# Down products of a feed-forward in seven half-width products instead of eight full-width tiles, in the last two of four sweeps

## The chip, the cores and the metric

The kernel runs on one core of a Trainium2 chip. The metric is the device time of one execution in microseconds; the median of several runs is compared. A profiled execution is one of its own, with its own time.

## The reference

For 8 x 512 tokens of 512 channels, in f32: attention with 16 heads of 32 channels (causal, softmax), added to its input and normalised over the channels; then a gated feed-forward, again added and normalised:

```python
gate = xt @ Wg.T ; up = xt @ Wu.T          # 4096 hidden values, weights unpacked from 4-bit codes and scales
gelu = tanh(0.7978845608 * (gate + 0.044715 * gate**3)) * gate * 0.5 + gate * 0.5
out = (gelu * up) @ Wd.T                   # back to 512 channels
```

## The kernel before

**Work and tiles.** An attention phase runs first, batch by batch, and the feed-forward phase overlaps its tail. The feed-forward is `feed_forward_phase`, and the change lies in it alone. It goes over the 4096 tokens in 4 sweeps (`NS`) of 1024 tokens (two tiles t of 512), and in each sweep over the 4096 hidden values in 16 groups (`NG`) of 256 (two halves m of 128). One group in one sweep is a quad, numbered j = 0 to 63; sweeps 3 and 4 are j = 32 to 47 and 48 to 63. In sweep 1 the weights of each group are unpacked, split in a high and a low float32r part and written to `w_scratch`; in the later sweeps they are read back from there.

**Precision.** Every product of f32 matrices is three matmuls in float32r (`three`, lines 1036 to 1040): high by high, high by low, low by high. A matmul has its own weight load.

**Gate and up** are made by a seven-product scheme for 2 x 2 blocks: 7 products per matrix and quad (`p1` to `p7`), each over two halves of the 256 + 256 input channels, so six matmuls of 512 columns, 84 for both matrices. Sums of input blocks (`sum_x`, `x_next`) and of weights (`sum_w`) are made beforehand; ACT copies banks between products (`seed`, `take_u2`, `take_u3`) and DVE adds them (`make_c22`, `seed_e`). ACT then does the gelu into `hid` (four blocks of 128 x 512, index 2m + t), DVE multiplies by up in place (`times_up`, hid_done), ACT copies the product to its float32r high part (`split_high`, inter_high) and POOL subtracts it to get the low part (`split_low`, inter_split).

**Down.** The down product of quad j - 1 is made during quad j (`down`, lines 1087 to 1107): for each of 8 subtiles of 128 tokens, six matmuls of 512 columns (two halves m, three passes), stationary `inter`, moving `wd`, into one of two banks `d_bank[n % 2]`. It waits for the low parts of its tokens, for the weights, and for DVE to have added the tile two before into the accumulator `acc` (`add_down`, lines 1421 to 1429, d_added).

**Order.** Each engine's order is written out by hand in its `rest()`, one pass of the loop for each quad; engines meet only at semaphores. PE's pass is:

```python
p1(j, "g"), p1(j, "u"), down(j - 1, 0), p6(j, "g"), p2(j, "g"), p6(j, "u"), p2(j, "u"), down 1, down 2,
p7, p5 "g", down 3, p7, p5 "u", down 4, p4 "g", p4 "u", down 5, p3 "g", p3 "u", down 6, down 7
```

(lines 1139 to 1161). SP issues all transfers (`rest`, lines 992 to 1031): in pass j, once all products of quad j - 1 are done, `wg` and `wu` of quad j + 1, and once the down product of quad j - 2 is done, `wd` of quad j + 1 (1 MB). At the first two quads of a sweep DVE takes the statistics of the finished tokens (`statistics`, `refine`), POOL normalises them to `out_stage`, and SP stores them and loads the residual of the next tokens to `acc`. At the last quad of a sweep (j % 16 == 15) DVE, ACT and POOL make the next sweep's inputs (`sum_x`, `x_part`, `x_low`).

## Time and profile before

| | us |
|---|---|
| median of 3 runs (lowest, highest) | 2690.54 (2690.24, 2692.3) |
| the profiled execution | 2689.03 |
| its span, first to last instruction | 2687.2 |
| PE busy (share of the span) | 2629.9 (98%) |
| DVE busy | 1555.0 (58%) |
| ACT busy | 1103.5 (41%) |
| POOL busy | 825.7 (31%) |
| mean granted clock of PE, share of full | 0.993 |

Busy time is a sum over an engine's instructions, over all stages. Matmuls are pipelined: one of 512 columns is shown with 0.39 us while the next starts sooner, so the interval between starts is the measure of the pace. PEld is the weight load, which runs beside matmuls.

### The profile page before, as it was taken

What the parts mean: (1) busy time and instruction counts of PE and PEld (TensorE: products, weight loads), DVE (VectorE), ACT (ScalarE), POOL (GpSimd) and SP (SyncE); (2) the same over time, 40 slices, a digit from 0 to 9 for tenths busy, and PEclk for the clock granted to TensorE, in tenths of its full rate; (3) what the DMA queues carried; (4) which work ended last, traced back from release to release, by engine and by line L of the source; (5) the groups of instructions that cost most, each with busy time, mean ns of one, the idle gap of its engine ahead of it and who ended that gap; (6) DMA issues with size and microseconds to landing.
All of it is one profiled execution on the core that took longest, in us unless ns stands there. A gap on an engine that the chain in (4) does not pass through costs nothing.

```text
span 2687.2 us, 37714 instructions
## 1 busy us (share of the span) xinstructions
PE 2629.9 (98%) x13314; PEld 2148.2 (80%) x13314; DVE 1555.0 (58%) x3224; ACT 1103.5 (41%) x2518; POOL 825.7 (31%) x992
## 2 busy tenths in 40 slices
PE   7999999999789999999999999999999999999998
PEld 6777887778468888888888888888888888888886
DVE  5777777777789888876333333633333363333334
ACT  4666666666644444443222222322222232222221
POOL 2444444443634443434111111321111132111112
PEclk9999999999899999999999999999999999999999
DMA  9666876768365655565444333554344345433441
GB/s 251 188 178 178 215 212 174 190 187 233 105 250 216 225 208 204 205 262 232 163 180 189 156 141 145 210 201 172 143 182 169 141 160 229 167 141 141 182 171 48
DMA packets 143085, 493.52 MB, mean 184 GB/s; under 512 B 11568, under 2 KB 48560, under 8 KB 118320
## 3 DMA queue, kind: packets, MB, share of 16 engines
q1 hardware_dynamic: 142896, 491.11, 53.2%
q8 instruction: 106, 1.74, 0.3%
q14 instruction: 83, 0.68, 0.1%
HBM read 356.84 MB, written 134.22 MB: 183 GB/s over the span
## 4 chain that ended last, share of the span: by engine, by line
PE 71%; DVE 1%; DMA 1%; issue 1%; ACT 0%; POOL 0%; SPq 0%; POOLq 0%; DVEq 0%; ACTq 0%
PE bank L1038 23%; PE bank L1039 23%; PE bank L1040 23%; PE bank L452 0%; DMA scale<-down_scales 0%; DMA x1T_scratch<-x_late 0%; DVE bstats L1486 0%; PE bank L438 0%; DVE acc L1429 0%; ACT probs L562 0%; PE bank L462 0%; PE bank L419 0%; ACT bx_h L1169 0%; DVE bits L1389 0%; DVE y L708 0%
## 5 line engine op out<-in xcount | busy, mean ns | idle before, releaser
L1648 POOL TENSOR_TENSOR inter_l<-hid,inter_h 128x512 fp32r<-128x512 f32 x256 | 338.0, 1321 | 1361.5 <-ACT inter_h L1169 1361.5
L1429 DVE TENSOR_TENSOR acc<-acc,bank 128x512 f32<-128x512 f32 x512 | 350.0, 685 | 331.8 <-PE bank L1040 322.8
L1038 PE MATMUL bank<-wd,inter_h 128*128 128x512 f32 x1024 | 399.7, 390 | 6.2 <-DVE acc L1429 5.2
L1039 PE MATMUL bank<-wd,inter_h 128*128 128x512 f32 x1024 | 398.9, 390 | 0.0
L1040 PE MATMUL bank<-wd,inter_l 128*128 128x512 f32 x1024 | 398.9, 390 | 0.0
L743 POOL TENSOR_SCALAR probs<-probs,row_inv 128x128 f32<-128x128 f32 (+3 forms) x512 | 264.4, 538 | 363.1 <-DVE row_inv L664 363.1
L1448 DVE TENSOR_TENSOR hid<-hid,bank 128x512 f32<-128x512 f32 x192 | 131.8, 687 | 397.1 <-PE bank L1040 395.4
L1038 PE MATMUL bank<-bx_h,wg 128*128 128x512 f32 x896 | 349.4, 390 | 0.9 <-ACT u_g L1169 0.9
L1039 PE MATMUL bank<-bx_l,wg 128*128 128x512 f32 x896 | 349.1, 390 | 0.0
L1040 PE MATMUL bank<-bx_h,wg 128*128 128x512 f32 x896 | 349.1, 390 | 0.0
L1038 PE MATMUL bank<-bx_h,wu 128*128 128x512 f32 x896 | 348.7, 389 | 0.0
L1040 PE MATMUL bank<-bx_h,wu 128*128 128x512 f32 x896 | 348.6, 389 | 0.0
L1039 PE MATMUL bank<-bx_l,wu 128*128 128x512 f32 x896 | 348.5, 389 | 0.0
L562 ACT ACTIVATE probs<-probs,neg_max 128x128 f32<-128x128 f32 (+3 forms) x512 | 281.7, 556 | 0.0
L675 DVE CUSTOM_DVE_ANT_0 probs<-bank,mask 128x128 f32<-128x128 f32 (+3 forms) x512 | 243.9, 481 | 26.2 <-PE bank L430 21.6
L1169 ACT ACTIVATE inter_h<-hid 128x512 fp32r<-128x512 f32 x256 | 160.6, 628 | 220.1 <-PE bank L1040 119.9
L438 PE MATMUL bank<-ident,probs 128*128 128x128 f32 x1280 | 228.3, 278 | 13.9 <-POOL probs L743 6.2
L1038 PEld LDWEIGHTS bank<-wd,inter_h 128*128 128x128 f32 x1024 | 192.5, 188 | 48.7 <-issue 5.3
L1237 ACT ACTIVATE hid<-bank 128x512 f32<-128x512 f32 x192 | 114.7, 597 | 269.7 <-PE bank L1040 197.3
L1040 PEld LDWEIGHTS bank<-wd,inter_l 128*128 128x128 f32 x1024 | 192.5, 188 | 40.1
L1039 PEld LDWEIGHTS bank<-wd,inter_h 128*128 128x128 f32 x1024 | 192.5, 188 | 39.6
L430 PE MATMUL bank<-k_st,q_st 128*128 128x256 f32 (+2 forms) x512 | 209.8, 410 | 12.4 <-DVE neg_max L675 7.0
(139 smaller groups left out, 4357.9 us busy)
## 6 DMA issues: line engine op xcount, KB each, us to landing
wg<-w_scratch SPq DMA_DIRECT2D x48, 1792.0 KB, 9.0
wu<-w_scratch SPq DMA_DIRECT2D x48, 1792.0 KB, 12.9
wd<-w_scratch SPq DMA_DIRECT2D x48, 1024.0 KB, 4.9
q_st<-qk_scratch SPq DMA_DIRECT2D x128, 256.0 KB, 5.0
k_st<-qk_scratch SPq DMA_DIRECT2D x128, 256.0 KB, 6.9
w_scratch<-wg SPq DMA_DIRECT2D x16, 1792.0 KB, 8.2
w_scratch<-wu SPq DMA_DIRECT2D x16, 1792.0 KB, 10.0
qk_scratch<-q_stage SPq DMA_DIRECT2D x32, 512.0 KB, 3.6
```

The lines of the kernel that those rows point to most:

```text
L430: pe.matmul(s_bank[k % 2][:, 0:n], q_st[:, st, g, k * P:(k + 1) * P], k_st[:, st, g, 0:n], start=True, stop=True).then_inc(s_done, 1)
L438: last = pe.transpose(t_bank[k % 2][:, (i - k) * P:(i - k + 1) * P], probs[:, h % 4, PCOL[i] + k * P:PCOL[i] + (k + 1) * P], ident[:])
L562: act.activation(p, p, ACT.Exp, bias=neg_max[:, h % 4, k:k + 1], scale=-1.0, accum_out=row_sum[:, h % 4, k:k + 1]).then_inc(exp_done, 1)
L675: dve.tensor_tensor_reduce(probs[:, s % 4, PCOL[k]:PCOL[k] + n], s_bank[k % 2][:, 0:n], mask[:, SEQ - n:SEQ], -SCALE, 3.0e38, ALU.add, ALU ...
L743: pool.tensor_scalar(p, p, row_inv[:, h % 4, k:k + 1], 1.0, ALU.mult, ALU.mult).then_inc(norm_done, 1)
L1038: pe.matmul(out, a(0), b(0), start=start, stop=False, skip_group_check=True)
L1039: pe.matmul(out, a(0), b(1), start=False, stop=False, skip_group_check=True)
L1040: return pe.matmul(out, a(1), b(0), start=False, stop=stop, skip_group_check=True)
L1169: return act.activation(out, in_, ACT.Copy)
L1429: dve.tensor_tensor(a, a, d_bank[n % 2][:, :], ALU.add).then_inc(d_added, 1)
L1448: dve.tensor_tensor(h, h, u_of(m, t), ALU.mult).then_inc(hid_done, 1)
L1648: pool.tensor_tensor(inter[1][:, m, t, :], hid[:, 2 * m + t, :], f32(inter[0][:, m, t, :]), ALU.subtract).then_inc(inter_split, 1)
```

## The change

In 28 quads, those with `seven(j)` (j = 33 to 46 and 49 to 62), the down product is made by the seven-product scheme too. Its 2 x 2 blocks are: tokens t by hidden halves m on one side, hidden halves m by halves of the 512 output channels on the other. Each product i has one hidden operand (128 x 512 tokens) and one weight operand (128 x 256). A step is one product for 256 tokens: two token tiles, each with three matmuls of 256 columns, into the two halves of one bank. Steps 0 to 6 are products 0 to 6 for the first 256 tokens of each tile, steps 7 to 13 for the second. A bank accumulates over steps where `FRESH` doesn't start it anew: products share partial sums in PSUM, and each step's bank is added to the accumulator's half rows that `ADD_TO` names.

- PE does the steps in pairs between pairs of products (`with_steps`).
- DVE makes four sums of hidden blocks (`hidden_sums`, around the adds of steps 12 and 13) and adds 14 steps; ACT and POOL split seven operands in high and low parts (`operand_high`, `operand_low`) where four were split.
- The four sums of down weights are made once, in sweep 2 (14 quads, `summed(j)`): POOL adds the two parts and makes the sums (`sums_of_down`), ACT and POOL split them, SP stores 1 MB for each to a new scratch `t_scratch` (`store_t`).
- In sweeps 3 and 4 SP loads seven weight operands of 256 KB for each such quad into `b_slot` (over `wd`), each when its slot is free (`load_operands`), in place of 1 MB of `wd`. `wd` of other quads is loaded one pass later than before (`load_down`).
- `sum_x` is cut in four calls, which DVE places between adds in quad 47. Other tiles lie over buffers that are idle then.

The core of the diff (the semaphores, the waits of `gelu`, and the rest of the orders, which follow the same pattern, are left out):

```diff
+HALF = HID // 2
+ADD_TO = ((0, 0), (0, 0), (0, 1), (1, 1), (1, 1), (0, 1), (1, 0))
+FRESH = (0, 1, 3)
+WEIGHT_OF = {0: (0, 0), 1: (1, 0), 5: (1, 1)}
+SUM_OF = {2: 0, 3: 1, 4: 2, 6: 3}
+PLACE_OF = {(0, 0): 0, (1, 0): 1, (0, 1): 4, (1, 1): 6}
...
+    spare = [plan(f"spare{n}", [P, TILE], F32R) for n in range(3)]
+    d_whole = plan("d_whole", [P, 2, HID], F32, over="w32_d")
+    t_sum = plan("t_sum", [P, 4, HALF], F32, over="spare0")
+    t_parts = plan("t_parts", [P, 4, 2, HALF], F32R, over="out_stage")
...
+    s1_parts = [plan(f"s1_{n}", [P, TILE], F32R, over="w32_d", skip=4 * TILE * i) for i, n in enumerate("hl")]
+    s4_low = plan("s4_l", [P, TILE], F32R, over="wd_0", skip=3 * 8 * HALF)
+    hid_sum = plan("hid_sum", [P, 2, TILE], F32, over="w_sum_g")
+    b_slot = [plan(f"b_slot{i}", [P, 2, HALF], F32R, over="wd_1" if i < 4 else "wd_0", skip=i % 4 * 8 * HALF)
+              for i in range(7)]
...
+    def seven(j):
+        return j >= 2 * NG and 0 < j % NG < NG - 1
+    def summed(j):
+        return j - NG if NG < j < 2 * NG - 1 else 0
+    def whole_loads(j):
+        return (j - NG) // 2 + 1 if j < 2 * NG else NG // 2 + j // NG - 1
+    def sevens(j):
+        return sum(seven(i) for i in range(j))
+    def steps(j):
+        return 8 * j + 6 * sevens(j)
+    def parts(j):
+        return 4 * j + 3 * sevens(j)
+    def place_free(j, i):
+        if seven(j - 1):
+            return steps(j - 1) + 7 + i + 1
+        return down_at(j - 1, 0, 3) if i < 2 else steps(j)
+    def part(i, l):
+        for (m, t), place in PLACE_OF.items():
+            if place == i:
+                return inter[l][:, m, t, :]
+        return {2: spare[l], 3: s1_parts[l], 5: (spare[2], s4_low)[l]}[i][:, :]
+    def operand(i):
+        return {0: hid[:, 0, :], 1: hid[:, 2, :], 2: hid_sum[:, 1, :], 3: hid_sum[:, 0, :], 4: hid[:, 1, :],
+                5: hid[:, 2, :], 6: hid[:, 3, :]}[i]
...
+        def store_t(j):
+            sp.wait_ge(t_split, j)
+            sp.dma_start(t_dram[j], f32(t_parts[:, :, :, :])).then_inc(t_stored, 16)
+        def load_down(j):
+            sp.wait_ge(down_done, steps(j - 1) + (11 if seven(j - 1) else 0))
+            if summed(j - 2):
+                sp.wait_ge(d_made, summed(j - 2))
+            load_w(j, 2)
+        def load_operands(j, a, b):
+            for i in range(a, b):
+                if seven(j - 1):
+                    sp.wait_ge(down_done, place_free(j, i))
+                else:
+                    sp.wait_ge(down_done, steps(j - 1) if i < 4 else steps(j))
+                if i in WEIGHT_OF:
+                    m, c = WEIGHT_OF[i]
+                    sp.wait_ge(w_stored[2][j % 2], 16 * (NG // 2))
+                    src = w_dram[j % NG, :, 2 * GU_W:].rearrange("p (l m h) -> p l m h", l=2, m=2)[
+                        :, :, m, c * HALF:(c + 1) * HALF]
+                else:
+                    sp.wait_ge(t_stored, 16 * (NG - 2))
+                    src = t_dram[j % NG, :, SUM_OF[i], :, :]
+                sp.dma_start(f32(b_slot[i][:, :, :]), src).then_inc(b_loaded[i], 16)
...
+                if st and not seven(j) and not seven(j - 1):
+                    load_down(j)
+                if summed(j - 2):
+                    store_t(summed(j - 2))
+                if seven(j) and not seven(j - 1):
+                    load_operands(j, 0, 4)
...
+                if seven(j):
+                    load_operands(j, 0 if seven(j - 1) else 4, 7)
+                elif seven(j - 1):
+                    load_down(j)
...
+        def step(j, n):
+            i, half = n % 7, n // 7
+            if half == 0:
+                pe.wait_ge(inter_split, parts(j) + i + 1)
+                pe.wait_ge(b_loaded[i], 16 * (sevens(j) + 1))
+            pe.wait_ge(d_added, steps(j) + n - 1)
+            for q in range(2):
+                tokens = slice((2 * half + q) * P, (2 * half + q + 1) * P)
+                last = three(d_bank[n % 2][:, q * HALF:(q + 1) * HALF], lambda l: part(i, l)[:, tokens],
+                             lambda l: b_slot[i][:, l, :], i in FRESH and q == 0, True)
+            last.then_inc(down_done, 1)
+        def with_steps(j):
+            p1(j, "g")
+            p1(j, "u")
+            step(j - 1, 0)
+            step(j - 1, 1)
+            p6(j, "g")
+            p2(j, "g")
+            step(j - 1, 2)
+            step(j - 1, 3)
...
+            step(j - 1, 12)
+            step(j - 1, 13)
...
+        def operand_high(j, i):
+            if i in (0, 1, 6):
+                act.wait_ge(hid_done, chain(j, *{0: (0, 0), 1: (1, 0), 6: (1, 1)}[i]))
+            else:
+                act.wait_ge(hid_summed, 4 * sevens(j) + {3: 1, 2: 2, 4: 3, 5: 4}[i])
+            act.wait_ge(down_done, place_free(j, i))
+            copy(part(i, 0), operand(i)).then_inc(inter_high, 1)
+        def sums_of_down_high(n):
+            act.wait_ge(t_summed, 4 * n)
+            if n > 1:
+                act.wait_ge(t_stored, 16 * (n - 1))
+            else:
+                act.wait_ge(out_stored, 32)
+            copy(t_parts[:, :, 0, :], t_sum[:, :, :]).then_inc(t_high, 1)
+        def with_operands(j, last):
+            st = j // NG
+            seed(j, "g")
+            seed(j, "u")
+            operand_high(j - 1, 2)
+            operand_high(j - 1, 3)
+            take_u2(j, "g")
+            operand_high(j - 1, 4)
+            operand_high(j - 1, 5)
+            gelu(j, 0, 0)
+            operand_high(j - 1, 6)
...
+        def add_step(j, n):
+            i, half = n % 7, n // 7
+            t, c = ADD_TO[i]
+            dve.wait_ge(down_done, steps(j) + n + 1)
+            if i in (1, 4):
+                dve.wait_ge(d_added, steps(j) + n)
+            a = acc[:, SUB * t + 2 * half:SUB * t + 2 * half + 2, c * HALF:(c + 1) * HALF]
+            dve.tensor_tensor(a, a, d_bank[n % 2][:, :].rearrange("p (a n) -> p a n", a=2), ALU.add).then_inc(d_added, 1)
+        def hidden_sums(j, first):
+            a11, a21, a12, a22 = (hid[:, n, :] for n in range(4))
+            s1, s2 = hid_sum[:, 0, :], hid_sum[:, 1, :]
+            done = 4 * sevens(j)
+            if first:
+                dve.wait_ge(hid_done, chain(j, 0, 1))
+                if seven(j - 1):
+                    dve.wait_ge(inter_split, parts(j - 1) + 4)
+                dve.tensor_tensor(s1, a21, a22, ALU.add).then_inc(hid_summed, 1)
+                dve.wait_ge(hid_summed, done + 1)
+                dve.tensor_tensor(s2, s1, a11, ALU.subtract).then_inc(hid_summed, 1)
+            else:
+                dve.tensor_tensor(a21, a11, a21, ALU.subtract).then_inc(hid_summed, 1)
+                dve.wait_ge(inter_split, parts(j) + 2)
+                dve.wait_ge(hid_summed, done + 2)
+                dve.tensor_tensor(a12, a12, s2, ALU.subtract).then_inc(hid_summed, 1)
+        def between(j):
+            if seven(j - 2) and seven(j - 1):
+                add_step(j - 2, 12)
+            if seven(j - 1):
+                hidden_sums(j - 1, True)
+            if seven(j - 2) and seven(j - 1):
+                add_step(j - 2, 13)
+            if seven(j - 1):
+                hidden_sums(j - 1, False)
+        def with_steps(j, last):
+            st = j // NG
+            add_step(j - 1, 0)
+            add_step(j - 1, 1)
+            if last:
+                sum_x(st + 1, x_next, 0)
+            add_step(j - 1, 2)
+            add_step(j - 1, 3)
...
+            make_c22(j, "g")
+            seed_e(j, "g")
+            add_step(j - 1, 6)
+            add_step(j - 1, 7)
...
+        def operand_low(j, i):
+            pool.wait_ge(inter_high, parts(j) + i + 1)
+            pool.tensor_tensor(part(i, 1), operand(i), f32(part(i, 0)), ALU.subtract).then_inc(inter_split, 1)
+        def sums_of_down(j, n):
+            pool.wait_ge(w_loaded[2][j % 2], 16 * whole_loads(j))
+            if n > 1:
+                pool.wait_ge(t_split, n - 1)
+            pool.tensor_tensor(d_whole[:, :, :], f32(wd[j % 2][:, 0, :, :]), f32(wd[j % 2][:, 1, :, :]),
+                               ALU.add).then_inc(d_made, 1)
+            pool.wait_ge(d_made, n)
+            w = d_whole
+            b11, b12, b21, b22 = (w[:, m, c * HALF:(c + 1) * HALF] for m in range(2) for c in range(2))
+            t2, t1, t3, t4 = (t_sum[:, n, :] for n in range(4))
+            pool.tensor_tensor(t1, b12, b11, ALU.subtract).then_inc(t_summed, 1)
+            pool.tensor_tensor(t3, b22, b12, ALU.subtract).then_inc(t_summed, 1)
+            pool.wait_ge(t_summed, 4 * n - 3)
+            pool.tensor_tensor(t2, b22, t1, ALU.subtract).then_inc(t_summed, 1)
+            pool.wait_ge(t_summed, 4 * n - 1)
+            pool.tensor_tensor(t4, b21, t2, ALU.subtract).then_inc(t_summed, 1)
+        def sums_of_down_low(n):
+            pool.wait_ge(t_high, n)
+            pool.tensor_tensor(t_parts[:, :, 1, :], t_sum[:, :, :], f32(t_parts[:, :, 0, :]),
+                               ALU.subtract).then_inc(t_split, 1)
```

## Rows read from the trace of the kernel before

**Rows 1.** The page, part 1: busy us, share, instructions.

```profile
PE 2629.9 (98%) x13314; PEld 2148.2 (80%) x13314; DVE 1555.0 (58%) x3224; ACT 1103.5 (41%) x2518; POOL 825.7 (31%) x992
```

**Rows 2.** Windows: each engine's busy us (instructions), PEclk, DMA share, GB/s.

```profile
1755.00:2205.00 450.00, 450.00 (x1986) 372.60 (x1985) 176.47 (x252) 129.77 (x219) 86.90 (x64) 1.00 0.42 166
2205.00:2650.00 445.00, 445.00 (x1965) 368.44 (x1964) 164.41 (x261) 120.72 (x207) 84.14 (x69) 1.00 0.41 161
```

**Rows 3.** Waits of PE, 1250 to 2687 us: total us, times, longest.

```profile
PE bank L1038 <- DVE acc L1429: 0.5, 2, 0.3
```

**Rows 4.** Timeline of PE, sweep 4: start us, us, instruction.

```profile
2200.05 0.39 PE L1038 MATMUL bank<-bx_h,wg 128*128 128x512 f32 x1
...
2225.89 0.39 PE L1038 MATMUL bank<-wd,inter_h 128*128 128x512 f32 x1
```

**Rows 5.** Timeline of PE in attention.

```profile
302.40 0.28 PE L419 MATMUL bank<-w_h,x_h 128*128 128x256 f32 x1
...
303.11 0.60 PE L438 MATMUL bank<-ident,probs 128*128 128x128 f32 x4
...
307.00 0.28 PE L419 MATMUL bank<-w_h,x_h 128*128 128x256 f32 x1
...
307.72 0.60 PE L438 MATMUL bank<-ident,probs 128*128 128x128 f32 x4
...
311.59 0.40 PE L419 MATMUL bank<-wo_h,a_h 128*128 128x512 f32 x1
...
312.29 0.60 PE L438 MATMUL bank<-ident,probs 128*128 128x128 f32 x4
```

**Rows 6.** Timeline of the weight loads in attention.

```profile
302.40 0.19 PEld L419 LDWEIGHTS bank<-w_l,x_h 128*128 128x128 f32 x1
302.52 0.19 PEld L419 LDWEIGHTS bank<-w_h,x_l 128*128 128x128 f32 x1
```

**Rows 7.** Groups by line and form: busy, mean ns, idle before.

```profile
L1648 POOL TENSOR_TENSOR inter_l<-hid,inter_h 128x512 fp32r<-128x512 f32 x256 | 338.0, 1321 | 1361.5 <-ACT inter_h L1169 1361.5
...
L1642 POOL TENSOR_TENSOR w_sum_g<-w_g,w_sum_g 128x256 f32<-128x256 f32 x16 | 17.0, 1062 | 1.3
...
L1637 POOL TENSOR_TENSOR w_sum_u<-w_u 128x256 f32<-128x256 f32 x16 | 12.3, 770 | 11.4 <-DVE w_u L1402 8.0 <-PE bank L452 3.4
...
L1657 POOL TENSOR_TENSOR x_first<-x_first,x_first 128x1024 f32<-128x1024 f32 x4 | 9.5, 2384 | 3.7 <-DMA x_first<-x1T_scratch 3.7
...
L1429 DVE TENSOR_TENSOR acc<-acc,bank 128x512 f32<-128x512 f32 x512 | 350.0, 685 | 331.8 <-PE bank L1040 322.8 <-DMA acc<-x_scratch 9.1
...
L1380 DVE TENSOR_TENSOR bx_l<-x_next,bx_h 128x1024 fp32r<-128x1024 f32 x12 | 24.8, 2069 | 0.0
...
L1376 DVE TENSOR_TENSOR x_next<-x_next,x_next 128x1024 f32<-128x1024 f32 x3 | 3.7, 1226 | 0.1
...
L1169 ACT ACTIVATE inter_h<-hid 128x512 fp32r<-128x512 f32 x256 | 160.6, 628 | 220.1 <-PE bank L1040 119.9 <-DVE hid L1448 100.2
...
L1169 ACT ACTIVATE bx_h<-x_next 128x1024 fp32r<-128x1024 f32 x21 | 21.4, 1048 | 0.0
```

**Rows 8.** Timeline of PE and ACT in sweep 3.

```profile
1916.42 0.39 PE L1038 MATMUL bank<-bx_h,wg 128*128 128x512 f32 x1
...
1917.97 0.58 ACT L1169 ACTIVATE bank<-bank 128x512 f32<-128x512 f32 x1 [4.84 <-PE bank L1040]
1919.34 0.58 ACT L1169 ACTIVATE bank<-bank 128x512 f32<-128x512 f32 x1 [0.78 <-PE bank L1040]
```

**Rows 9.** Timeline of SP, and DMA issues: count, KB, median us to landing.

```profile
2215.88 0.33 SPq L950 DMA_DIRECT2D wd<-w_scratch  x1
...
2245.80 0.33 SPq L950 DMA_DIRECT2D wd<-w_scratch  x1
...
wu<-w_scratch SPq DMA_DIRECT2D x48, 1792.0 KB, 12.9
wd<-w_scratch SPq DMA_DIRECT2D x48, 1024.0 KB, 4.9
```

More of the change, by code:

```diff
@@ L887, in down_at @@
     def down_at(j, t, q):
-        return 8 * j + 4 * t + q + 1
+        return steps(j) + 4 * t + q + 1
     FIRST_X = (0, 2, 4, 6, 1, 3, 5)
@@ L1557, in rest @@
                 ends, ended = j and j % NG == 0, j % NG == 1 and j > NG
+                between(j)
+                if seven(j - 1):
+                    with_steps(j, last)
+                    continue
                 if prep and j > 1:
@@ L1576, in rest @@
                 if last:
-                    sum_x(st + 1, x_next)
+                    for n in range(4):
+                        sum_x(st + 1, x_next, n)
                 make_c22(j, "g")
@@ L1729, in rest @@
                     sum_w(j + 1, 0)
-                split_low(j - 1, 1, 1)
-                split_low(j - 1, 0, 1)
+                if seven(j - 1):
+                    for i in range(2, 7):
+                        operand_low(j - 1, i)
+                else:
+                    split_low(j - 1, 1, 1)
+                    split_low(j - 1, 0, 1)
+                if summed(j - 1):
+                    sums_of_down(j - 1, summed(j - 1))
                 if ended:
@@ L1736, in rest @@
                     sum_w(j + 1, 1)
-                split_low(j, 0, 0)
+                if seven(j):
+                    operand_low(j, 0)
+                else:
+                    split_low(j, 0, 0)
                 if ends:
```

143 lines of the change are left out of this document (120 added, 23 removed).

## The prediction

> **What bounds the kernel now.** I read the profile from the outside in. The page's first part has PE at 98% of the span, every other engine at 58% or less [rows 1]. The windows say where the few idle microseconds are: in the last two sweeps, which the change rewrites, PE is busy for all of 450 and all of 445 us, at a granted clock of 1.00, which is the 2.4 GHz level; DVE is busy 39% there, ACT 29%, POOL 19% and the DMA queues 41% [rows 2]. The list of waits from 1250 us on has PE behind anything for 0.5 us in all [rows 3]. So in these sweeps the time is the number of matmuls times the interval between their starts. That interval is in PE's timeline: from 2200.05 to 2225.89 us there are 114 intervals of 512-column matmuls, 0.2267 us each [rows 4]. A quad has 84 of them for gate and up and 48 for down: 132 x 0.2267 = 29.92 us, and the loads of `wd` stand exactly 29.92 us apart [rows 9]. Where a wait bounded PE, fewer columns would return nothing; here each column taken from PE returns its time, as long as the other engines deliver.
>
> **PE's term.** 28 quads (33 to 46 and 49 to 62) change. Each loses 48 down matmuls of 512 columns (10.88 us) and gets 7 products x 4 token tiles x 3 passes = 84 of 256 columns: 21504 columns for 24576, but 36 more instruction pairs. No 256-column matmul runs in these sweeps, so its interval has to be bounded. Attention has them, of the same operand types, in threes. Two runs of six take 0.71 and 0.72 us, 0.118 and 0.120 each [rows 5]. In the same stretch three 512-column matmuls take 0.70 us, 0.233 each, 3% over the feed-forward's 0.2267; what adds those 6 ns there I cannot see. If it is a share, 256 columns cost 0.119 x 0.2267 / 0.233 = 0.116 here; if it is a constant, 0.113, which is also exactly half of 0.2267; if it belongs to the half width alone, 0.119. I take **0.116**: 84 x 0.116 = 9.74 us, a gain of 1.14 us a quad, 31.9 us over 28. The ends: 0.113 gives 9.49 and 38.9 us, 0.120 (the slower run) gives 10.08 and 22.4 us. Break-even is at 10.88 / 84 = 0.1295.
>
> Weight loads grow from 48 to 84. A load lasts 0.19 us in the trace, longer than the 0.116 us of its matmul, but loads of the same shape start every 0.12 us and lie across each other [rows 6], so they set no longer interval than the one used. The Trainium skill, TensorE: Matmul & The Clock Gate, section "The mechanism" of its part on packing, states that a weight load overlaps matmuls in flight only where the row groups differ. All loads here use the whole array, so by that rule each of the 36 added loads would stand bare, 36 x 0.19 = 6.8 us a quad, and the change would lose. The trace disagrees: 512-column matmuls with a load each start every 0.2267 us [rows 4], where 512 columns at 2.4 GHz are 0.213. A milder form of it is the first rival below.
>
> **The new quad's timetable.** Product = six 512-column matmuls = 1.36 us, a pair of steps = 1.39. With 0 at the start of p1 gate: p1 ends at 2.72; steps 0, 1 end at 3.42, 4.11; p6, p2 gate to 6.83; steps 2, 3 start at 6.83, 7.53; p6, p2 up to 10.94; steps 4, 5; p7, p5 gate 12.34 to 15.06; steps 6, 7; p7, p5 up to 19.17; steps 8, 9; p4 20.56 to 23.28; steps 10, 11; p3 24.68 to 27.40; steps 12, 13 to 28.79. An engine starts 0.19 us after PE's end: p1 at 1916.42 plus 1.36 gives 1917.78, the seed starts at 1917.97, and the second at 1919.34 [rows 8].
>
> ACT and POOL: the two seeds end at 3.5. Behind them ACT now makes the high parts of operands 2 and 3 (0.63 each, to 4.1 and 4.7), later 4, 5 and 6. POOL's low parts take 1.32 each [rows 7]: operand 2 at 5.5, operand 3 at 6.8, then 8.3, 9.6, 10.9. Steps 2 to 6 want them at 6.83, 7.53, 10.94, 11.64 and 15.06. The nearest margin is 0.7 us, at step 3. Operands 0 and 1 are made in the quad before (low part of 1 at 26.3, wanted 5 us later). ACT has 3 x 0.63 us more a quad and POOL 3 x 1.32: hidden.
>
> DVE: 14 adds for 8, 6 x 0.69 = 4.1 us more [rows 7] (the same 512 elements, though in two half rows; I take the same price), and four sums of hidden values. These have two SBUF inputs: half of a 1024-element one (1.23) is 0.61; a subtraction of the same size and with two SBUF inputs took 2.07, 1.7 times that, in the quads that stage inputs [rows 7], so 1.04 is the upper end. In order: product by up (0,1) from 27.59, add of step 12 to 28.97, two sums to 30.3, add 13 to 31.0, two sums to 32.3, which is 3.5 into the next quad; that quad's add 0 can start at 3.61. The steps that wait: step 0 for add 12 (29.0 against 31.5), step 1 for add 13 (31.0 against 32.2), step 10 for add 8 (22.1 against 23.3), step 11 for add 9 (22.8 against 24.0). The least margin is 1.1 us; with sums at 1.04, add 13 comes at 31.9, still in time. Hidden. ACT's operand 2 wants its sum at 3.5 and has it at 1.5.
>
> SP and DMA: 1 MB of `wd` becomes seven loads of 256 KB, 1.75 MB. At a share of 41% that adds some 7 points. Slot i is free after step 7 + i (16.5 to 28.8) and wanted at 31.5 or later; the least gap is over 11 us against 4.9 to landing for all of `wd` [rows 9]. SP stands at step 13 at the end of an iteration, so the gate and up loads, now behind `wd`'s place, go out some 1.4 us later; landing takes 13 us and the matmul is 28 us away. `wd` of quads 47 and 63 now waits for step 10 of the quad before (about 24): landed at 29, wanted at 31.5, 2.5 us to spare. Nothing is added.
>
> **Sweep 2** (14 quads): POOL gets one 1024-element sum (2.4), four of 256 (0.77 to 1.06) and one low part (2 x 1.32 = 2.6), 8 to 9 us; ACT one 1024-element copy of 1.05 us [rows 7]; SP a store of 1 MB. POOL is 81% idle in the sweeps shown, and the split queued behind the sums, (0,0) of the running quad, ends near 18 and is wanted 15 us later. The last low part ends under 1 us into the next quad, before that quad's first split (about 7). Cost 0.
>
> **Quad 47**, where the next sweep's inputs are staged: DVE has 14 adds, 8 other operations on 512 columns, the hidden sums, 4 sums of 1.23 and 4 low parts of 2.07, 31 us in a quad of 28.8. Following its queue, add 8 ends at 23.3 and add 9 at 24.0, just when steps 10 and 11 want them; adds 10 and 11 end at 27.4 and 28.1, again at the edge for steps 12 and 13; add 12 ends at 31.6 against 31.5. I charge 0.7 us once (0 to 3).
>
> **Sum.** 31.9 - 0.7 = 31.2 us. The profiled execution took 2689.0 us around a span of 2687.2, and stands 1.5 below the median of 2690.5; 2657.8 for it, so **2659.3** for the median.
>
> **The rivals.**
> 1. Exposed or slow weight loads: with half the columns per load, loads come to set the pace at their own 0.188 us: 84 x 0.188 = 15.8, plus 4.9 us a quad, 138 us slower, near 2828. The runs of six and the overlapping loads are against it [rows 5, 6]. The Trainium skill's rule named above is for it. 2%.
> 2. Slower through one place: POOL's low parts between ACT's operand 3 and step 3. POOL's sums of the same size differ that much in sweep 1 (0.77 against 1.06 for 256 elements) [rows 7]. If low parts beside the denser DVE queue took 2.6 in place of 1.32, operand 3 would come at 9.4 against 7.53, operand 5 at 14.6 against 13.5 (shifted): 3 us a quad lost, 1.14 won, 52 us slower, near 2742. It decides from 0.7 us of lateness and turns the sign at 1.8. Against: POOL's 256 splits average 1.32 through all stages, and DVE's neighbours there read PSUM. 5%.
> 3. The change gives nothing: a 256-column matmul with waits around each six costs 0.127 to 0.131, or waits eat the gain; 2690 within 5.4. 256-column runs that end in a wait show no such extra (the sixth interval, to the transposes, is in the 0.71 above). 4%. That the steps don't replace the old tiles is excluded by the diff.
> 4. Half gains: PE's term holds but each pair waits some 0.4 us, at the operands or the adds: 11 us lost, near 2671. 12%.
> 5. The forecast, 77%, 2651 to 2669 from PE's ends.
>
> The range holds the forecast and most of rival 4: 2650 to 2673. What a measurement can tell from no change is 0.2%, 5.4 us; faster takes cases 4 and 5, 0.89; same 0.04; slower 0.07.
>
> **What would show it.** The timeline of a quad in 33 to 46: 256-column starts 0.116 apart and `wd` or first-product starts 28.8 us apart; PE busy through the windows of sweeps 3 and 4. Wrong if the spacing is 0.118 or more without waits (PE's term mis-sized), if PE's waits list names POOL's low part or DVE's add at steps, or if sweep 2's quads leave 29.92. Matmul intervals that differ from 0.2267 for 512 columns in the new quads would also break the sum.

## The result, and the profile after

| kernel | runs | median us | lowest to highest |
|---|---|---|---|
| before | 4 | 2690.39 | 2688.05 to 2692.30 |
| changed | 4 | 2673.55 | 2672.84 to 2674.77 |

The ratio is 0.9938, with a 95% interval of 0.9921 to 0.9955: 16.8 us faster, or 0.62%. The forecast was 31.2 us, with 2650 to 2673 as its range, so the sign was right and the size about half. The profiled execution of the changed kernel took 2674.77 us around a span of 2672.9.

The page's first part of the changed kernel, against [rows 1]:

```profile
span 2672.9 us, 41044 instructions
PE 2612.9 (98%) x14322; PEld 2177.0 (81%) x14322; DVE 1739.2 (65%) x3504; ACT 1154.1 (43%) x2616; POOL 1044.4 (39%) x1160
```

PE executes 1008 more matmuls (36 in each of 28 quads) in 17.0 us less busy time. The windows of sweeps 2, 3 and 4 answer to [rows 2]:

```profile
1300.00:1755.00 455.00, 453.89 (x2001) 374.97 (x2000) 184.20 (x276) 142.77 (x232) 205.03 (x158) 1.00 0.52 198
1755.00:2205.00 450.00, 450.00 (x2531) 394.82 (x2530) 274.95 (x410) 151.03 (x264) 146.94 (x112) 1.00 0.55 192
2205.00:2650.00 445.00, 444.84 (x2508) 390.62 (x2507) 258.05 (x397) 142.45 (x254) 136.19 (x109) 1.00 0.54 186
```

PE is still full in sweeps 3 and 4 and its clock is at the 2.4 GHz level there. DVE went from 39% to 61% (274.95 of 450), POOL from 19% to 33%, the DMA share from 0.42 to 0.55. None of them became a bound in these windows as a whole. In sweep 2 PE misses 1.1 of 455 us, where before it was busy for all 455. PE's list of waits from 1250 to 2672 us, against [rows 3], names where:

```profile
PE bank L1140 <- DVE acc L1647: 1.4, 3, 0.7
PE bank L1140 <- DMA wd<-w_scratch: 0.2, 1, 0.2
```

Line 1647 is the add of a whole down tile, which is not used for the products of the 28 new quads, and the wait for `wd` comes behind the last of them. So the new quads have no listed wait at all, and yet they gained too little. ACT's seeds give the length of a quad:

```profile
1917.99 0.58 ACT L1316 ACTIVATE bank<-bank 128x512 f32<-128x512 f32 x1 [3.58 <-PE bank L1142]
1947.25 0.58 ACT L1316 ACTIVATE bank<-bank 128x512 f32<-128x512 f32 x1 [3.58 <-PE bank L1142]
```

1947.25 - 1917.99 = 29.26 us, and so are all 26 distances that lie wholly in the two stretches of new work (quads 34 to 46 and 50 to 62, each of which executes the down product of the quad before it; the last of each stretch, executed in quads 47 and 63, comes below). Before it was 29.92; the forecast was 28.78. PE's timeline inside such a quad (its seed is that of 1888.73), against [rows 4, 5], has the reason:

```profile
1902.43 0.28 PE L1140 MATMUL bank<-b_slot,inter_h 128*128 128x256 f32 x1
1902.54 0.28 PE L1141 MATMUL bank<-b_slot,inter_h 128*128 128x256 f32 x1
1902.66 0.28 PE L1142 MATMUL bank<-b_slot,inter_l 128*128 128x256 f32 x1
...
1903.86 0.40 PE L1140 MATMUL bank<-bx_h,wu 128*128 128x512 f32 x1
...
1905.25 0.39 PE L1140 MATMUL bank<-bx_h,wu 128*128 128x512 f32 x1
...
1906.61 0.28 PE L1140 MATMUL bank<-b_slot,inter_h 128*128 128x256 f32 x1
```

Three intervals matter. A pair of steps, 12 matmuls of 256 columns, takes 1903.86 - 1902.43 = 1.43 us, 0.119 each: the first interval is 0.11, the others are 0.12. The first six matmuls of 512 columns behind it take 1.39 us, 0.232 each. The next six take 1.36, the old 0.2267. A quad has seven such groups and seven times 0.03 us of the slower sixes: 7 x 1.43 + 7 x 2.75 = 10.01 + 19.25 = 29.26. The gain is 0.66 us a quad, 18.5 over 28.

The other loss is one place, quad 31, the last of sweep 2. Its seed and that of quad 32, and PE's two longer waits between them:

```profile
1679.93 0.58 ACT L1316 ACTIVATE bank<-bank 128x512 f32<-128x512 f32 x1 [3.89 <-PE bank L1142]
1712.04 0.59 ACT L1316 ACTIVATE bank<-bank 128x512 f32<-128x512 f32 x1
```

```profile
1706.46 0.50 PE L1140 MATMUL bank<-wd,inter_h 128*128 128x512 f32 x1 [0.41 <-DVE acc L1647]
1708.80 0.50 PE L1140 MATMUL bank<-wd,inter_h 128*128 128x512 f32 x1 [0.68 <-DVE acc L1647]
```

The distance is 32.11 us (29.95 before), and the next 29.73 (29.91 before): 2.0 us lost in all. (The seed of quad 32 comes some 0.2 us behind PE, as ACT is still busy with copies; so quad 31 looks 0.2 too long and quad 32 as much too short.) The two listed waits add up to 1.09 us, yet they and one that is not listed cost PE the 2.0: the last matmul before each stop starts 0.41, 0.80 and 1.07 us ahead of the next in place of 0.2267, and the first one behind each stop 0.33 or 0.34 ahead of the second. A listed wait counts only from the modelled end of the matmul before it. DVE's timeline shows the sums of the next sweep's inputs, and the list of instructions that write `t_sum` shows POOL's sums of weights beside them (minimum, median and maximum ns, first and last start):

```profile
1691.42 6.27 DVE L1594 TENSOR_TENSOR x_next<-x_next,x_next 128x1024 f32<-128x1024 f32 x4
```

```profile
L1973 POOL TENSOR_TENSOR t_sum<-d_whole x14: 731/735/1597, 1302.7 to 1691.6; 128x256 f32<-128x256 f32 x14
L1974 POOL TENSOR_TENSOR t_sum<-d_whole x14: 740/742/1720, 1303.4 to 1693.2; 128x256 f32<-128x256 f32 x14
```

Before, DVE's four sums took 4.9 us. Here they take 6.27 (one 1.23, three 1.64), while POOL's four take 1.6 to 1.7 in place of 0.74 each. In the other 13 quads of sweep 2 DVE has no such sums, and POOL's stay at their median.

**The account.** 18.5 us from the new quads, less 2.0 at quad 31. Quad 47 went from 29.99 to 29.45, 0.1 less than its share. From the seed of quad 63 to the end the kernels took 51.07 us before and 51.16 after, where a new quad's gain of 0.66 should lie: 0.75 lost. Of this, 0.40 is gone by PE's last matmul (40.26 us behind the seed before, 40.00 after, where 0.66 less was due), and belongs to the late `wd` (below). The other 0.35 lies behind SP's last store instruction, from which the kernel needed 4.5 us to its end before and 4.9 after. That makes 15.6. Between the two profiled executions 1.3 us of it is missing, since the seed of quad 31 came at 1678.59 before and 1679.93 after, with every quad of sweep 2 ahead of it at 29.92 in both. Over the runs below, nearly all of which have the changed kernel's code up to there, that seed comes between 1677.17 and 1682.04, and once at 1678.59 exactly, so this is a spread of the stages ahead. 15.6 - 1.3 is the 14.3 between the spans; the medians are 16.8 apart.

### The profile page after: what moved, and what is told of

It reads as the page before. It is cut to its first block, busy times and chain, and to the rows that moved or that the text cites. A ratio compares the mean times of both kernels' runs of the same rounds, so it can differ in the third digit from the quotient of the medians.

```text
span 2672.9 us, 41044 instructions
## 1 busy us (share of the span) xinstructions
PE 2612.9 (98%) x14322; PEld 2177.0 (81%) x14322; DVE 1739.2 (65%) x3504; ACT 1154.1 (43%) x2616; POOL 1044.4 (39%) x1160
## 4 chain that ended last, share of the span: by engine, by line
PE 70%; DVE 2%; DMA 1%; issue 1%; POOL 0%; ACT 0%; SPq 0%; POOLq 0%; DVEq 0%; ACTq 0%
PE bank L1140 23%; PE bank L1141 23%; PE bank L1142 23%; PE bank L452 0%; PE bank L438 0%; DVE acc L1647 0%; DMA x1T_scratch<-x_late 0%; DMA scale<-down_scales 0%; DVE bx_l L1598 0%; DVE bstats L1788 0%; POOL probs L743 0%; DMA wd<-w_scratch 0%; DVE hid L1750 0%; PE bank L419 0%; PE bank L462 0%
## 5 line engine op out<-in xcount | busy, mean ns | idle before, releaser
L1657 DVE TENSOR_TENSOR acc<-acc,bank 128x512 f32<-128x512 f32 x392 | 263.4, 684 | 94.3 <-PE bank L1142 84.3
L1647 DVE TENSOR_TENSOR acc<-acc,bank 128x512 f32<-128x512 f32 x288 | 196.5, 684 | 143.5 <-PE bank L1142 135.6
L1140 PE MATMUL bank<-wd,inter_h 128*128 128x512 f32 x576 | 225.7, 392 | 7.5 <-DVE acc L1647 6.1
L1142 PE MATMUL bank<-wd,inter_l 128*128 128x512 f32 x576 | 224.7, 390 | 0.0
L1141 PE MATMUL bank<-wd,inter_h 128*128 128x512 f32 x576 | 224.6, 390 | 0.0
L438 PEld LDWEIGHTS bank<-ident,probs 128*128 128x128 f32 x1280 | 160.9, 142 | 64.3 <-POOL probs L743 10.0
```

The lines of the kernel that those rows point to most:

```text
L438: last = pe.transpose(t_bank[k % 2][:, (i - k) * P:(i - k + 1) * P], probs[:, h % 4, PCOL[i] + k * P:PCOL[i] + (k + 1) * P], ident[:])
L1140: pe.matmul(out, a(0), b(0), start=start, stop=False, skip_group_check=True)
L1141: pe.matmul(out, a(0), b(1), start=False, stop=False, skip_group_check=True)
L1142: return pe.matmul(out, a(1), b(0), start=False, stop=stop, skip_group_check=True)
L1647: dve.tensor_tensor(a, a, d_bank[n % 2][:, :], ALU.add).then_inc(d_added, 1)
L1657: dve.tensor_tensor(a, a, d_bank[n % 2][:, :].rearrange("p (a n) -> p a n", a=2), ALU.add).then_inc(d_added, 1)
```

## Experiments

Lengths of quads are distances of ACT's seeds. The kernel before beside each group of runs took 2689.75, 2689.25 and 2690.39 us (the last a median of 9). Experiments 1 to 7 and 10 are one execution each. With a spread of several us in the stages ahead, what they say rests on the lengths of quads, which repeat to 0.01 or 0.02 us in nearly all of them, and less on the total.

**1. The same products with whole rows.** Each step as three matmuls of 512 columns for 128 tokens in place of six of 256.

```diff
-            for q in range(2):
-                tokens = slice((2 * half + q) * P, (2 * half + q + 1) * P)
-                last = three(d_bank[n % 2][:, q * HALF:(q + 1) * HALF], ...
+            tokens = slice(2 * half * P, (2 * half + 1) * P)
+            last = three(d_bank[n % 2][:, :], lambda l: part(i, l)[:, tokens],
+                         lambda l: b_slot[i][:, :, :].rearrange("p l n -> p (l n)"), i in FRESH, True)
```

> The changed kernel with each step as three matmuls of 512 columns instead of six of 256: the same columns, half the matmuls and weight loads, the same adds, waits and operands. It leaves out the second token tile of each step and mixes the weight's two parts, so its output is not the reference's. Theory A (a matmul costs a fixed part of some 6 ns beside its columns while it is short or follows short ones): the quad falls from 29.26 us to 126 x 0.2267 = 28.56, about 19 us less in all, near 2655. Theory B (the missing time lies in waits or in what the steps' banks and operands cost): the quad stays at 29.26 and the time at 2674.

2657.64 us; a quad is 28.56 us, which is 126 x 0.2267 to the last digit. PE's timeline:

```profile
1901.44 0.39 PE L1140 MATMUL bank<-b_slot,inter_h 128*128 128x512 f32 x1
...
1902.80 0.39 PE L1140 MATMUL bank<-bx_h,wu 128*128 128x512 f32 x1
...
1905.52 0.39 PE L1140 MATMUL bank<-b_slot,inter_h 128*128 128x512 f32 x1
```

The six matmuls of a pair of steps take 1.36 us and the twelve of two products 2.72. Waits, operands, adds and transfers are those of the changed kernel, and in these quads they cost nothing even at 28.56. So the whole shortfall of the quads, in the steps and behind them, comes from the form of the steps: twelve matmuls of 256 columns with twelve loads, in place of six of 512 with six loads. Width and number change together here, and this run doesn't part them. The shortfall is worth 0.70 us a quad, 19.6 us. The total is 3 us above the 2655 expected, since quad 31's seed came at 1682.04 and quad 47 took 29.06. There POOL's low part of operand 3 runs beside one of DVE's sums of inputs and takes 2.28 us in place of 1.30, and PE's weight load waits for it:

```profile
2148.89 2.28 POOL L1959 TENSOR_TENSOR s_l<-hid_sum,s_h 128x512 fp32r<-128x512 f32 x1
```

```profile
2151.22 0.19 PEld L1140 LDWEIGHTS bank<-b_slot,s_h 128*128 128x128 f32 x1 [0.49 <-POOL s_l L1959]
```

How to have this gain with all tokens, by steps whose moving side is 512 wide, was not tried.

**2. Shorter weight loads.** The stationary operand is cut to 64 columns, the moving one stays at 256.

```diff
-                tokens = slice((2 * half + q) * P, (2 * half + q + 1) * P)
-                last = three(d_bank[n % 2][:, q * HALF:(q + 1) * HALF], ...
+                tokens = slice((2 * half + q) * P, (2 * half + q) * P + 64)
+                last = three(d_bank[n % 2][0:64, q * HALF:(q + 1) * HALF], ...
```

> The changed kernel with the stationary operand of each step's matmuls 64 columns wide instead of 128; the number of matmuls and the 256 moving columns stay. Half of each token tile is left out, so its output is not the reference's. Theory A1 (the weight load of 128 columns holds a 256-column matmul at 0.119 us): the interval in steps falls to 0.113 and the quad to about 28.6 to 28.8. Theory A2 (the extra belongs to every matmul in such a stretch, whatever is loaded): interval 0.119, quad 29.26.

2659.58 us, a quad 28.79. PE's timeline:

```profile
1902.24 0.28 PE L1140 MATMUL bank<-b_slot,inter_h 128*64 128x256 f32 x1
...
1903.61 0.40 PE L1140 MATMUL bank<-bx_h,wg 128*128 128x512 f32 x1
...
1904.99 0.39 PE L1140 MATMUL bank<-bx_h,wu 128*128 128x512 f32 x1
```

The twelve now take 1.37 us, 0.114 each. Averaged over the quads from 1800 to 2100 us, the first two intervals are 0.118 and 0.117 and the others 0.1133, half of a 512-column one, where the changed kernel has 0.12. So what holds the short matmuls at 0.12 goes with the 128-column stationary operand. Its weight load is the likely part, but the output shrinks from 128 to 64 rows with it, and no run parts the two. The six matmuls behind still take 1.38: that loss is not of the stationary operand's width.

**3. One step at a time.** Steps 0 to 11 stand alone between single products, and 12 and 13 stay together: 13 places in place of 7.

```diff
-            step(j - 1, 0)
-            step(j - 1, 1)
-            p6(j, "g")
-            p2(j, "g")
+            step(j - 1, 0)
+            p6(j, "g")
+            step(j - 1, 1)
+            p2(j, "g")
...
```

> The changed kernel with PE's steps one by one between single products (13 places) instead of in pairs between pairs of products (7 places); the same instructions otherwise. Theory A (the six 512-column matmuls that follow short ones cost 0.2317 instead of 0.2267 each, however many short ones came): six more slow products a quad, 6 x 0.03 = 0.18 us, quad 29.44, about 5 us slower in all. Rival (the extra belongs to the number of short matmuls): quad 29.26.

2676.68 us, a quad 29.38. PE's timeline:

```profile
1900.33 0.40 PE L1140 MATMUL bank<-bx_h,wg 128*128 128x512 f32 x1
...
1901.72 0.28 PE L1140 MATMUL bank<-b_slot,inter_h 128*128 128x256 f32 x1
...
1902.43 0.40 PE L1140 MATMUL bank<-bx_h,wu 128*128 128x512 f32 x1
```

Now 13 of the 14 products stand behind a step and take 1.39 us, the other one 1.36; the twelve single steps take 0.71 each and the pair 1.43: 18.07 + 1.36 + 8.52 + 1.43 = 29.38. The slowness is a toll of each passage from short to long matmuls, paid over the first six behind it, and not a share of all. The quad stays 0.06 below the 29.44 expected because each of the six new places begins with a short interval of 0.11.

**4. The sums of inputs spread out.** In quad 31 three of DVE's four sums go between earlier adds.

```diff
+                early = last and j > NG
+                if early:
+                    sum_x(st + 1, x_next, 0)
                 add_down(j - 1, 0)
+                if early:
+                    sum_x(st + 1, x_next, 1)
...
+                if early:
+                    sum_x(st + 1, x_next, 2)
                 add_down(j - 1, 1)
...
-                    for n in range(4):
+                    for n in range(3 if early else 0, 4):
```

> The changed kernel with DVE's four sums of the next sweep's inputs in quad 31 spread between its adds, as the change itself does in quad 47, instead of in one block beside POOL's sums of down weights. Theory (DVE and POOL slow each other there, and DVE comes late to the adds): quad 31 falls from 32.1 us to 30.0 to 30.6, about 2 us less in all. Rival (POOL's or ACT's longer queue holds quad 31): it stays at 32.1.

2671.43 us. Quad 31 takes 29.92 in place of 32.11, and quad 32 29.92 too. DVE's timeline where the four sums were:

```profile
1690.08 2.23 DVE L1594 TENSOR_TENSOR x_next<-x_next,x_next 128x1024 f32<-128x1024 f32 x1
1692.23 0.68 DVE L1736 TENSOR_TENSOR u_g<-bank,u_g 128x512 f32<-128x512 f32 x1
```

The one sum left beside POOL's sums takes 2.23 us, against 1.22 before, and the third takes 1.60 beside POOL's first sum, which takes 3.39 in place of 2.39; neither delays PE. This run had the same front as the kernel before (quad 31's seed at 1678.59 in both), so their spans can be set side by side: 2687.2 - 2669.6 = 17.6, which is 18.5 less quad 47 and the end.

**5. Long and short one by one.** The matmuls of steps 1 to 12 alternate with those of the twelve products behind them.

```diff
+            waits_of_step(with_step)
             for c in range(2):
-                last = three(out[:, :], ...)
+                for k, (l, r) in enumerate(PASSES):
+                    last = pe.matmul(out[:, :], w[:, l, A_SLOT[i], c, :], ...)
+                    matmul_of_step(with_step, 3 * c + k)
```

> The changed kernel with the six 256-column matmuls of steps 1 to 12 laid one by one between the six 512-column matmuls of the products p6 to p3 (512, 256, 512, 256, ...); steps 0 and 13 stay whole. Same matmuls, same operands, same result. Theory L (a 128-column weight load takes some 0.12 us and a load can run ahead only a little, so short matmuls in a row wait for it and a long one between them lets it catch up): a pair costs 0.1133 + 0.2267 = 0.340 us and the quad falls to about 28.6, 18 us less in all, near 2656. Theory S (each matmul near a short one costs some 5 ns more, whatever the order): a pair costs 0.351 and the quad is 29.4 or more. Between them, a pair at 0.12 + 0.2267 (the load before each matmul has only that one matmul to hide behind): 29.1.

2712.84 us, a quad 30.3 to 30.6: slower than the kernel before. PE's timeline, and its list of waits from 1800 to 2140 us:

```profile
1900.22 0.40 PE L1157 MATMUL bank<-bx_h,wu 128*128 128x512 f32 x1
1900.46 0.28 PE L1182 MATMUL bank<-b_slot,s_h 128*128 128x256 f32 x1
...
1902.34 0.40 PE L1157 MATMUL bank<-bx_h,wu 128*128 128x512 f32 x1
```

```profile
PE bank L1157 <- DVE acc L1673: 6.3, 11, 0.6
```

Six pairs take 2.12 us, 0.353 each. That is 0.232 + 0.119 and a little more, near theory S: beside a long matmul the short one costs no less, and each long one now pays its toll. Theory L, by which the short ones would catch up, is out. 72 pairs and the 24 left over make 29.6 us; the rest are waits for adds (6.3 / 11, or 0.6 a quad) and what follows them. This was meant to beat both kernels and is the slowest run of all.

**6. No sums of down weights in sweep 2.** POOL makes, ACT copies and SP stores nothing more there than before the change. (The edit that lets sweeps 3 and 4 load stored down weights in place of the sums is left out.)

```diff
...
     def summed(j):
-        return j - NG if NG < j < 2 * NG - 1 else 0
+        return 0
...
```

> The changed kernel without the sums of down weights in sweep 2: no POOL sums, splits and stores there, and in sweeps 3 and 4 all seven weight operands are read from the stored down weights, so four products use the wrong weights and the output is not the reference's. Theory (POOL's sums beside DVE's sums of inputs cost the 2.2 us of quad 31, and nothing else in sweep 2): quad 31 back to 29.95, the other quads as in the changed kernel. Rival (quad 31's 2.2 us come from the later loads of the down weights): it stays at 32.1.

2671.76 us. Quad 31 takes 30.03 and quad 32 29.92, all other quads as in the changed kernel. DVE's four sums at that place:

```profile
1690.52 5.00 DVE L1594 TENSOR_TENSOR x_next<-x_next,x_next 128x1024 f32<-128x1024 f32 x4
```

5.00 us, near the 4.9 before the change. The later loads of `wd` stay, so they are not the cause. ACT's copy and SP's store are gone with POOL's sums, but ACT's copy comes at 1710.14 in the changed kernel, long behind DVE's sums, and where POOL's work stays and most of DVE's moves away (experiment 4) the 2 us return as well. Experiments 4 and 6 each remove them, one from either side of the pair. The end is shorter here too: 4.6 us behind SP's last store instruction, as before the change, where the changed kernel and experiments 1 to 3 need 4.9. So 0.3 us of the end goes with the sums of down weights; by what, no run shows.

**7. Steps of 288 columns.** A little more work under each load.

```diff
-                last = three(d_bank[n % 2][:, q * HALF:(q + 1) * HALF], ...
+                last = three(d_bank[n % 2][:, q * 224:q * 224 + 288], ...
```

> The changed kernel with 288 columns in each matmul of a step instead of 256, overlapping by 32 columns a half, so the output is not the reference's. Theory L (interval = the larger of the weight load, 0.12, and 17/16 of a cycle a column, here 0.1275): 0.1275 to 0.128 in steps, 84 x 0.0083 = 0.7 us more a quad, and the 512-column matmuls behind them start at 0.2267 at once. Theory S (column time plus 6 ns): 0.1335, 1.2 us more a quad, and the matmuls behind the steps stay slow.

2699.71 us, a quad 30.15. PE's timeline:

```profile
1902.36 0.29 PE L1140 MATMUL bank<-b_slot,inter_h 128*128 128x288 f32 x1
...
1903.94 0.39 PE L1140 MATMUL bank<-bx_h,wg 128*128 128x512 f32 x1
...
1906.67 0.29 PE L1140 MATMUL bank<-b_slot,inter_h 128*128 128x288 f32 x1
```

0.1317 for a step's matmul, between the two expected values, where the share of 512 columns is 0.1275: at 288 columns a load of 128 is not hidden for nothing either. So the load is no plain floor. But the twelve behind take 2.73 us, 2.724 on average from 1800 to 2100 us, which is 0.004 over 12 x 0.2267 in place of 0.03. The toll all but goes as the short matmuls grow by an eighth. The neighbouring outputs overlap by 32 columns in this run, which no other run does; whether that adds to the price is open. Both readings of the step's price, a pure floor and a pure share, fall here.

**8 and 9. The changed kernel again, and the version of experiment 4.** Five rounds each on the same chip.

> The changed kernel once more, in five rounds, beside the next run on the same chip: 2673.5, 16 to 17 us below the kernel before. Both theories expect the same; it is the base for the next run.

> The changed kernel with the four sums of inputs in quad 31 spread between the adds, in five rounds. Its profile already had quad 31 at 29.92 us instead of 32.1. Theory (the 2.2 us return in full): 2671.3, ratio to the kernel before 0.9930 against 0.9938. Rival (later quads or the tail take it back): as the changed kernel.

| kernel | median us | lowest to highest | ratio to before, 95% |
|---|---|---|---|
| before (9 runs) | 2690.39 | 2689.24 to 2691.77 | |
| changed | 2674.66 | 2671.98 to 2675.28 | 0.9940, 0.9928 to 0.9953 |
| sums spread | 2672.46 | 2672.20 to 2674.28 | 0.9935, 0.9922 to 0.9949 |

The change's gain stands in a second measurement. Spreading the sums is 2.2 us better by medians. Quads 31 and 32 together are 2.0 us shorter (29.93 + 29.91 against 32.09 + 29.74). The theory's 2671.3 was 1.2 us too low, as was the 2673.5 for the changed kernel. The two intervals overlap, so the total alone doesn't show the gain; the quads' lengths do. It is the fastest version that computes everything.

**10. Groups of four steps.** Fewer passages from short to long: groups of 2, 4, 4 and 4 steps in place of seven pairs.

```diff
-            step(j - 1, 2)
-            step(j - 1, 3)
             p6(j, "u")
             p2(j, "u")
+            step(j - 1, 2)
+            step(j - 1, 3)
             step(j - 1, 4)
             step(j - 1, 5)
...
```

> The changed kernel with PE's steps in groups of two, four, four and four between groups of four products, instead of seven pairs. Theory (each return from short to long matmuls costs 0.03 us and each start of a short run saves 0.01; a step after two others waits for DVE's add, some 0.17 to 0.2 us, three times or more): four returns instead of seven save 0.06 to 0.09 us, the waits cost 0.5, quad 29.7. Rival (adds keep up): quad 29.2, 2 us less in all. The list of waits of PE then names DVE's adds or does not.

2708.32 us, a quad 30.27, quad 47 33.54. PE's timeline at the third step of a group, and the waits from 1800 to 2140 us:

```profile
1901.57 0.28 PE L1142 MATMUL bank<-b_slot,s_l 128*128 128x256 f32 x1
1902.00 0.35 PE L1140 MATMUL bank<-b_slot,inter_h 128*128 128x256 f32 x1 [0.16 <-DVE acc L1657]
```

```profile
PEld bank L1140 <- DVE acc L1657: 6.3, 23, 0.4
PEld bank L1140 <- issue: 3.6, 11, 0.3
PE bank L1140 <- DVE acc L1657: 1.9, 12, 0.2
```

The interval is 0.43 us where 0.12 is usual, and the next 0.19. There are two banks, a step takes 0.71 us, and an add takes 0.68 and starts 0.2 after its step: the third step of a group waits for DVE, the fourth hardly. The waits cost 0.37 us a group (24 short matmuls take 3.245 us on average from 1800 to 2100 us, where 0.11 + 23 x 0.12 is 2.87), 1.1 us a quad in place of the 0.5 expected. What three passages fewer save (0.03 us each) is lost many times over. With two banks and this add, pairs are the best of the three groupings measured.

## Why the prediction was wrong

**The step that failed: "PE's term".** I took 0.116 us for a 256-column matmul, between ends of 0.113 and 0.120; it measured 0.1192 (1.43 / 12). That is 84 x 0.0032 = 0.27 us a quad. Nearly as much lies in the form of the sum: it kept 84 x 0.2267 us for gate and up. Seven sixes of them, 42 matmuls, cost 0.2317: 42 x 0.005 = 0.21 us. The two make 0.48 us, the distance from 1.14 to 0.66, and 28 x 0.48 = 13.4 us. With 2.0 for quad 31 and 0.75 at the end, less 0.6 that quad 47 was overcharged, this is the 15.6 between the account and 31.2.

The warning stood in [rows 5]. Three 512-column matmuls in attention took 0.70 us, 0.233 each, and I wrote of the 6 ns that what adds them "I cannot see", then scaled the 256-column price down by that very share. In the new quads the first three long matmuls behind short ones take 0.70 us as well (1916.40 to 1917.10), and without short ones ahead nothing is slow (experiment 1). So the likely reading is that attention's three were slow because short ones stood ahead of them, and that the short ones were at their own price already: 0.118 to 0.120 was the value to take, unscaled. And a row in which the neighbours are slower in mixed company should have been carried over to the long matmuls of the new quads. With both, the same sum gives 10.88 - 84 x 0.119 - 42 x 0.005 = 0.67 us a quad, 18.8 us in all. The text named both signs in its last part (0.118 or more without waits; 512-column intervals that differ from 0.2267), but the range was made without the second. The measured 2673.55 lies just outside it.

**"Weight loads" were half right.** They don't stand bare, which the Trainium skill's rule would have had cost 6.8 us a quad. But the sentence that they "set no longer interval than the one used" failed: with a stationary operand of 64 columns the interval fell from 0.119 to 0.114 (experiment 2). The overlap of loads in [rows 6] shows that they are pipelined, not that they are free. The Trainium skill, TensorE: Matmul & The Clock Gate, section "LDWEIGHTS (loading the stationary operand)", gives a load P / 1.2 ns for P columns, by an estimate from it 107 ns for 128: less than 0.113, so that by it alone the load would hide. The measured 0.119, and 0.12 once the run is under way, disagrees if the load is what sets it, as experiment 2 makes likely; the measurement decides.

**"Cost 0" for sweep 2 failed at one of its 14 places.** It asked whether POOL had time for its sums, and whether what is queued behind them is late. POOL had the time. It did not ask who else works at that moment. In quad 31 DVE's sums with two SBUF inputs run beside POOL's, both slow down (1.22 to as much as 1.65 a sum on DVE, 0.74 to 1.6 or more on POOL), DVE's adds come late, and PE waits: 2.0 us. The Trainium skill, GPSIMD Engine Reference, section "1. Specifications", says that POOL shares its SBUF interfaces with DVE and contends with DVE instructions of two SBUF inputs; the trace and experiments 4 and 6 agree, and where DVE reads a PSUM bank instead, as in its adds, POOL's low parts kept their 1.30 us. I had this pair in the second rival, for sweeps 3 and 4, and not where it did harm.

The trace before already had its price. The 2.07 us of [rows 7] for DVE's low part of an input is a mean of two kinds, 2.9 where POOL does the same work beside it and 1.21 elsewhere, as DVE's timeline in quad 31 shows:

```profile
1696.79 2.92 DVE L1380 TENSOR_TENSOR bx_l<-x_next,bx_h 128x1024 fp32r<-128x1024 f32 x1
...
1703.04 1.21 DVE L1380 TENSOR_TENSOR bx_l<-x_next,bx_h 128x1024 fp32r<-128x1024 f32 x1
```

The prediction took the mean for the price of a subtraction. A mean far above the smallest of its group is a reason to look at the single instructions.

**Quad 47** was charged 0.7 us and cost 0.1. That is in part the longer quad's doing: at 28.79 a quad (experiment 2) it cost 0.27, at 28.56 (experiment 1) 0.5. Rival 2's place, and nearly its price, are real in it: the low part of operand 3 took 2.28 us there, where the rival had 2.6, but in this one of the new quads only, and in the changed kernel without a listed wait. **The end** was charged nothing: `wd` of quad 63 was to land at 29 and to be wanted at 31.5. SP's and PE's timelines:

```profile
2644.71 0.32 SPq L1045 DMA_DIRECT2D wd<-w_scratch  x1
```

```profile
2649.73 0.47 PE L1140 MATMUL bank<-wd,inter_h 128*128 128x512 f32 x1 [0.16 <-DMA wd<-w_scratch]
```

Quad 63's first product starts some 1.55 us ahead of its seed at 2621.74, at 2620.2. The issue comes 24.5 us behind it and the landing 5 us later, both about as forecast. But 31.5 counts the 2.72 us of the next quad's `p1` ahead of the down product, and behind quad 63 there is no next quad: `wd` is wanted at 28.8 in the forecast's own times. PE's listed wait is 0.16 us, and its true cost 0.4: the matmul starts 0.44 us behind the one before it in place of 0.12, and the one behind it 0.31 later in place of 0.2267. The other 0.35 of the 0.75 lies behind the last store instruction.

**What held.** The timetable of the quad: operand 3's low part ended at 1923.10 and step 3 started at 1924.04, a margin of 0.9 where 0.7 was given. No wait on adds, operands, DMA or SP in the new quads, in a quad of 29.26 and, outside quad 47, even in one of 28.56 (experiment 1). DVE's hidden sums took 0.69 each, inside 0.61 to 1.04. The DMA share did not hold: it rose by 13 points and not by 7, while the bytes rose as forecast (166 to 192 GB/s), so the new loads keep the queues busier for each byte; it cost PE nothing. The groups by line and form, against [rows 7], have the adds of two half rows and the low parts of the new quads at the prices taken, 0.69 and 1.32:

```profile
L1657 DVE TENSOR_TENSOR acc<-acc,bank 128x512 f32<-128x512 f32 x392 | 263.4, 684 | 94.3 <-PE bank L1142 84.3 <-DVE acc L1657 0.5
...
L1960 POOL TENSOR_TENSOR inter_l<-hid,inter_h 128x512 fp32r<-128x512 f32 x112 | 146.0, 1303 | 368.6 <-ACT inter_h L1316 368.6
```

So the rivals of waits (2 and 4) were wrong as accounts of the new quads, although the result landed near the time of rival 4: that is luck, half the gain without its waits. Rival 4's sum was wrong too: 11 us lost over 28 quads is 0.4 us a quad, and 0.4 at each of the seven pairs would be some 78 us. Rival 1 was far off in size, but if experiment 2's difference is the load's, loads do set part of the pace, as it had it.

## What to carry to other kernels

Halving a matmul's moving side from 512 to 256 columns did not halve its time while the stationary operand stayed at 128 columns (0.119 against 0.113 us), and it slowed the long ones behind it; price a new mixture of shapes by a row in which the same mixture stands, and carry what that row says of the neighbours too. Put short matmuls together in as long a run as the banks and the engine that empties them allow, and not one by one between long ones. Before work is given to an idle POOL, look at what DVE does at that moment, not only at POOL's share. And a listed wait of 0.16 us on PE can cost 0.4: measure it between starts.

## What the runs showed of the hardware

- In runs of twelve, a 256-column float32r matmul with a stationary operand of 128 columns starts every 0.119 us (first interval 0.11, then 0.12), with one of 64 every 0.114 (at first 0.118, then 0.1133); 288 columns with 128 every 0.132; 512 columns every 0.2267. The operand of 128 adds 5 ns at 256 columns; at 288 columns the price is 4 ns over the share of columns.
- After a run of such short matmuls the next six of 512 columns take 0.232 each, whether the short ones' stationary operands had 64 or 128 columns, and whether there were six or twelve of them; after 288 columns 4 of the 30 ns of a run's excess are left. With 512 and 256 in turn each pair takes 0.353. What state of PE this is stays open: no run looks inside it.
- DVE and POOL operations with SBUF operands alone slow each other when they run together: POOL's 256-element sum 0.74 to 1.6 or 1.7 us, DVE's 1024-element sum 1.22 to 1.64 in a row of four and to 2.23 for a single one, DVE's low part of an input 1.21 to 2.9, POOL's low part of an operand 1.30 to 2.28.
- Where PE stops for a wait, the second matmul behind the stop starts 0.31 to 0.34 us after the first in place of 0.2267 (512 columns).
